# Counts of edges in fp16 with two loads on their way, and all products of codes on VectorE: a graph layer on one core of Trainium2

## What is computed

```python
xn = layernorm(x)
deg_inv = 1 / max(segment_sum(ones, dst), 1)
sage(h) = h @ W_self + (segment_sum(h[src], dst) * deg_inv) @ W_neigh + b
gnn = sage1(relu(sage0(xn)))
Q, K, V = elu(xn@Wq+bq)+1, elu(xn@Wk+bk)+1, xn@Wv+bv
mix = gelu((Q * sum(K*V) / (Q * sum(K) + 1e-6)) @ Wo + bo)
x1 = x + gnn + mix
h = act_qdq(layernorm(x1))             # act_qdq: rounding to 16-bit codes, one scale for the whole tensor
up, gate = act_qdq(h @ qdq(w_up).T), act_qdq(h @ qdq(w_gate).T)
gate = act_qdq(gate * round_u16(sigmoid(gate)))
out = x1 + act_qdq(gate * up) @ qdq(w_down).T
```

## Time and profile before

| | us |
|---|---|
| median of 3 runs | 1245.42 |
| lowest, highest | 1242.05, 1246.09 |
| the profiled execution | 1242.91 |
| its span, first to last instruction | 1241.1 |
| TensorE busy in it | 1161.6 |
| granted TensorE clock, mean | 0.972 |

### The profile page before, as it was taken

The page is one execution under the profiler, slowest core; times in us unless marked ns, Lnnn a source line. Parts: engine busy times, 40 slices in busy tenths (PEclk is TensorE's granted clock), DMA queues, the critical chain, the costliest instruction groups (busy, mean ns, idle before and its releaser), DMA issues.

```text
span 1241.1 us, 15392 instructions
## 1 busy us (share of the span) xinstructions
PE 1161.6 (94%) x6376; PEld 626.5 (50%) x6376; DVE 683.4 (55%) x1225; ACT 355.5 (29%) x442; POOL 385.5 (31%) x213
## 2 busy tenths in 40 slices
PE   3969999999999999999999999999999999979848
PEld 2535455555555554444444555444444445469724
DVE  6569578665373583227334344666655355662653
ACT  5443333323333323312421122312110022243430
POOL 2047576768777685786000000000000000000010
PEclk8879999999999999999999999999999999989969
DMA  9963554342433437526670135213130130000004
GB/s 283 393 212 53 156 112 122 63 107 20 90 53 56 107 70 249 147 44 216 237 259 3 59 113 178 85 35 136 69 102 17 46 142 1 1 1 2 1 31 135
DMA packets 140718, 130.33 MB, mean 105 GB/s; under 512 B 74892, under 2 KB 114060, under 8 KB 139624
## 3 DMA queue, kind: packets, MB, share of 16 engines
q1 hardware_dynamic: 72072, 116.24, 27.8%
q0 software_dynamic: 68288, 12.98, 8.0%
q10 hardware_dynamic: 288, 0.13, 0.0%
HBM read 101.25 MB, written 27.72 MB: 104 GB/s over the span
## 4 chain that ended last, share of the span: by engine, by line
PE 45%; DMA 23%; POOL 13%; issue 12%; DVE 3%; ACT 2%; SPq 1%; POOLq 0%; DVEq 0%; ACTq 0%
PE ps L1035 21%; DMA at_scratch<-copies,cell 16%; POOL at_scratch L597 12%; PE ps L1097 7%; PE ps L1069 7%; PE ps L1122 6%; PE ps L1142 3%; DMA at_scratch<-zeros 3%; DMA raw<-in_L_gnn_W_neigh_dram 2%; DMA raw<-in_L_gnn_W_self_dram 1%; DMA parts<-at_scratch 1%; DVE AT L1240 1%; PE ps L1014 1%; SPq L398 1%; PE ps L1085 1%
## 5 line engine op out<-in xcount | busy, mean ns | idle before, releaser
L952 PE MATMUL ps<-xnT,whl 128*128 128x512 f16 (+1 forms) x2160 | 386.4, 342 | 13.1 <-ACT Qs L762 10.6
L597 POOL DMA_INDIRECT at_scratch<-copies,cell x160 | 342.0, 2137 | 176.1 <-DMA at_scratch<-copies,cell 93.5
L952 PEld LDWEIGHTS ps<-xnT,whl 128*128 128x128 f16 x2160 | 211.7, 99 | 185.6 <-issue 15.8
L1035 PE MATMUL ps<-hb,hT 128*128 128x512 f16 x960 | 209.1, 379 | 1.4 <-DVE hT L1493 1.4
L1035 PEld LDWEIGHTS ps<-hb,hT 128*128 128x128 f16 x960 | 93.6, 98 | 112.3 <-DVE hT L1493 1.8
L579 POOL PARTITION_ALL_REDUCE ag_fw<-am_fw x9 | 3.2, 354 | 369.2 <-DVE am_fw L1360 369.2
L1035 PE MATMUL ps<-hb,xnT 128*128 128x512 f16 x480 | 105.9, 383 | 0.0
L1035 PE MATMUL ps<-hb,VT 128*128 128x512 f16 x480 | 103.9, 379 | 1.5 <-ACT S_b L721 1.5
L1097 PE MATMUL ps<-P,AT 125*128 125x512 f16 x400 | 87.8, 379 | 0.0
L1069 PE MATMUL ps<-AT,P 125*128 125x512 f16 (+1 forms) x480 | 84.7, 339 | 0.0
L1122 PE MATMUL ps<-codeT,w 128*128 128x250 f16 x600 | 67.5, 275 | 9.5 <-DVE codeT L1613 7.6
(11 more groups left out here) (224 smaller groups left out, 1181.1 us busy)
## 6 DMA issues: line engine op xcount, KB each, us to landing
raw<-in_L_gnn_W_neigh_dram SPq DMA_DIRECT2D x32, 512.0 KB, 5.9
parts<-at_scratch SPq DMA_DIRECT2D x20, 625.0 KB, 5.0
raw<-in_L_gnn_W_self_dram SPq DMA_DIRECT2D x24, 512.0 KB, 5.5
at_scratch<-zeros POOLq DMA_DIRECT2D x12, 1020.0 KB, 18.7
key_b<-key_scratch SPq DMA_DIRECT2D x8, 1250.0 KB, 11.2
raw<-in_L_mix_Wo_dram SPq DMA_DIRECT2D x16, 512.0 KB, 3.8
x_all<-in_x_dram SPq DMA_DIRECT2D x9, 512.0 KB
x_acc<-in_x_dram SPq DMA_DIRECT2D x9, 512.0 KB
```

The source lines that it names most:

```text
L597: pool.indirect_dma_start(out=at_scr[c % 2][:, :], out_offset=bass.IndirectOffsetOnAxis(ap=cell[:, c:c + 1], axis=0), in_=copies[:, c:c + ...
L952: mm = pe.matmul(acc_of(c)[:, a:b], whl[:, i, wp, k, :], xnT[:, k, ap, a:b], start=(k == 0 and wp == 0 and ap == 0), stop=(k == KC - 1 and ...
L1035: mm = pe.matmul(half_bank(i), stationary[:, k, ap, t * TP:t * TP + P], hb[:, n % 2, k, wp, :], start=(k == 0 and wp == 0 and ap == 0), st ...
```

## The change

- at_scr, zeros, parts and copies are fp16. The tile zeros keeps its bytes, so three DMAs clear an array, not six.
- cells(p) counts to a new fp32 tile, counted. One more VectorE instruction for each p writes copies: the number where it is under 255.5, otherwise 0, as 256 and more would not stay exact in fp16 sums.
- There are four part tiles. Parts 0 to 5 alternate between two tiles over AT's tiles 6 to 9; parts 6 to 9 alternate between two over b1_b and bo_b. Load 1 waits for nothing, loads 2 to 5, 8 and 9 for the add of the part two before, load 6 for b1_ok as before, load 7 for VectorE's last mix_in. counts(6) and counts(8) wait for the add before them, since they write over a part tile.
- POOL makes no product. ACT codes blocks 1 and 2 of U in one step each (round_code), and VectorE multiplies all three blocks.

```diff
--- before.py
+++ after.py
@@ -49,7 +49,7 @@
     NPC = 8
     CPP = ET // NPC
     CELLS = P * 12240
-    NZ = 6
+    NZ = 3
     IC = I // P
     BLK = 32
     NBLK = D // BLK
@@ -146,8 +146,9 @@
         w_last = sb("w_last", [P, 2, D], F16, RG)
 
 
-        zeros = sb("zeros", [P, CELLS // (NZ * P)], F32, RD)
-        parts = [sb("parts0", [P, 2, NP], F32, RG), sb("parts1", [P, 2, NP], F32, RD + 6 * NP * 2)]
+        zeros = sb("zeros", [P, CELLS // (NZ * P)], F16, RD)
+        parts = [sb(f"parts{q}", [P, 2, NP], F16, o) for q, o in enumerate(
+            (RD + 6 * NP * 2, RD + 8 * NP * 2, RG, RG + NP * 4))]
 
         edge = Area(RG, RG + 5024)
         e_int = edge("e_int", [EH, 4, EP], I32)
@@ -158,6 +159,7 @@
         once = kept("once", [EP, EP], F32)
         again = kept("again", [EP, CPP], F32)
         spare = kept("spare", [EP, CPP], F32)
+        counted = kept("counted", [EP, CPP], F32)
         squared = kept("squared", [P, D], F16)
 
         key_b = sb("key_b", [P, 2, CPP * EP], F32, RE + 8192)
@@ -203,7 +205,7 @@
         stats2 = const("stats2", [P, 2, 6], F32)
         amax2 = const("amax2", [P, 2, NT + 1], F32)
         spare_c = const("spare_c", [EP, 1], F32)
-        copies = const("copies", [EP, ET], F32)
+        copies = const("copies", [EP, ET], F16)
         cell = const("cell", [EP, ET], I32)
 
         ps = ctx.enter_context(nc.psum_tensor("ps", [P, 4096], F32))
@@ -218,7 +220,7 @@
         s_scr = nc.dram_tensor("s_scratch", (D, N), F32, kind="Internal").ap()
         diag_scr = nc.dram_tensor("diag_scratch", (P * (P + 1),), F32, kind="Internal").ap()
         key_scr = nc.dram_tensor("key_scratch", (E,), F32, kind="Internal").ap()
-        at_scr = [nc.dram_tensor(f"at_scratch{b}", (CELLS, 1), F32, kind="Internal").ap() for b in range(2)]
+        at_scr = [nc.dram_tensor(f"at_scratch{b}", (CELLS, 1), F16, kind="Internal").ap() for b in range(2)]
         w_scr = nc.dram_tensor("w_scratch", (NF, P, 2 * D), F16, kind="Internal").ap()
 
         def sem(name):
@@ -235,7 +237,7 @@
         zero_out, key_out = [sem("zero_out0"), sem("zero_out1")], sem("key_out")
         key_in = [sem("key_in0"), sem("key_in1")]
         scattered = [sem("scattered0"), sem("scattered1")]
-        parts_in = [sem("parts_in0"), sem("parts_in1")]
+        parts_in = [sem(f"parts_in{q}") for q in range(4)]
         out_done = sem("out_done")
 
         diag_set, diag_out, ident_in = sem("diag_set"), sem("diag_out"), sem("ident_in")
@@ -272,7 +274,6 @@
         ug_done, ug_free = sem("ug_done"), [sem("ug_free0"), sem("ug_free1")]
         g_step, g_round, gs_step, gs_round, u_step, u_round, o_step, o_round = (
             sem(n) for n in ("g_step", "g_round", "gs_step", "gs_round", "u_step", "u_round", "o_step", "o_round"))
-        u_last = sem("u_last")
         gate_ok, sig_ok, o_code, o_hi, o_lo = (sem(n) for n in ("gate_ok", "sig_ok", "o_code", "o_hi", "o_lo"))
         dn_done, dn_free = sem("dn_done"), sem("dn_free")
 
@@ -380,7 +381,7 @@
 
         def part_of(s):
 
-            return (1, s) if s < 6 else (0, s - 6)
+            return (s % 2, s // 2) if s < 6 else (2 + s % 2, (s - 6) // 2)
 
         def half_index(w, part):
             return HALVES.index((w, part))
@@ -511,8 +512,10 @@
                         sp.wait_ge(scattered[b], 16 * (ET // 2))
                 elif s == 6:
                     sp.wait_ge(b1_ok, NT)
-                else:
-                    sp.wait_ge(at_ok, s)
+                elif s == 7:
+                    sp.wait_ge(m1_ok, 2 * NT)
+                elif s != 1:
+                    sp.wait_ge(at_ok, s - 1)
                 for b in range(2):
                     sp.dma_start(parts[q][:, b, 0:N],
                                  at_scr[b][s * TP * N:(s * TP + P) * N, :].rearrange("(p n) o -> p (n o)", n=N)
@@ -605,13 +608,8 @@
                 pool.tensor_tensor(x_acc[:TP, t, :], x_acc[:TP, t, :], b1_b[:TP, :], ALU.add).then_inc(b1_ok, 1)
             for j in range(NF):
                 ffn_max(j)
-            for e in (X2, MG, MGS, MU):
+            for e in (X2, MG, MGS, MU, MO):
                 whole(e)
-
-            c = IC - 1
-            pool.wait_ge(u_round, 1)
-            pool.tensor_tensor(G[:, cols(c)], U[:, cols(c)], G[:, cols(c)], ALU.mult).then_inc(u_last, 1)
-            whole(MO)
 
         @block.scalar
         def _(act):
@@ -886,12 +884,7 @@
             ug_out(2 * NR_F - 2)
             ug_out(2 * NR_F - 1)
             act.wait_ge(u_step, 1)
-
-            c = IC - 1
-            steps(act.activation(U[:, cols(c)], U[:, cols(c)], ACT.Identity, bias=pos_magic[:, :],
-                                 scale=sv[:, Q_U + 1:Q_U + 2]))
-            act.activation(U[:, cols(c)], U[:, cols(c)], ACT.Identity, bias=neg_magic[:, :]).then_inc(u_round, 1)
-            for c in range(1, IC - 1):
+            for c in range(1, IC):
                 round_code(U[:, cols(c)], Q_U, u_round)
             act.wait_ge(o_step, 1)
             for r, (a, b) in enumerate(OCOLS):
@@ -1222,11 +1215,12 @@
                     c = p * CPP + q
                     keys = key_b[:EP, p % 2, q * EP:(q + 1) * EP]
                     last = dve.scalar_tensor_tensor(keys, keys, key_c[:, c:c + 1], once[:, :], ALU.is_equal,
-                                                    ALU.mult, accum_out=copies[:, c:c + 1])
+                                                    ALU.mult, accum_out=counted[:, q:q + 1])
                 last.then_inc(key_used, 1)
                 dve.wait_ge(key_used, p + 1)
                 of = slice(p * CPP, (p + 1) * CPP)
-                dve.tensor_scalar(again[:, :], copies[:, of], 255.5, None, ALU.is_ge)
+                dve.tensor_scalar(again[:, :], counted[:, :], 255.5, None, ALU.is_ge)
+                dve.scalar_tensor_tensor(copies[:, of], counted[:, :], 255.5, counted[:, :], ALU.is_lt, ALU.mult)
                 steps(dve.tensor_scalar(spare[:, :], key_c[:, of], -1.0, spare_c[:, 0:1], ALU.mult, ALU.add))
                 steps(dve.tensor_tensor(spare[:, :], spare[:, :], again[:, :], ALU.mult))
                 dve.tensor_tensor(cell[:, of], spare[:, :], key_c[:, of], ALU.add).then_inc(cell_ok, 1)
@@ -1234,8 +1228,8 @@
             def counts(s):
 
                 q, k = part_of(s)
-                if s == 6:
-                    dve.wait_ge(at_ok, 6)
+                if s in (6, 8):
+                    dve.wait_ge(at_ok, s - 1)
                 dve.wait_ge(parts_in[q], 32 * (k + 1))
                 dve.tensor_tensor(AT[:, s, 0:N], parts[q][:, 0, 0:N], parts[q][:, 1, 0:N], ALU.add).then_inc(at_ok, 1)
                 if s == NT - 1:
@@ -1664,14 +1658,11 @@
                                     ALU.mult, ALU.mult))
             steps(dve.tensor_scalar(sv[:, TMP2:TMP2 + 1], sv[:, TMP:TMP + 1], 1 / 32767.0, None, ALU.mult))
             for c in range(IC):
-                if c + 1 < IC:
-                    if c > 0:
-                        dve.wait_ge(u_round, c + 1)
-                    code(U[:, cols(c)], Q_U, rounded=c > 0)
-                    steps(dve.scalar_tensor_tensor(G[:, cols(c)], U[:, cols(c)], MAGIC, G[:, cols(c)], ALU.subtract,
-                                                   ALU.mult))
-                else:
-                    dve.wait_ge(u_last, 1)
+                if c > 0:
+                    dve.wait_ge(u_round, c)
+                code(U[:, cols(c)], Q_U, rounded=c > 0)
+                steps(dve.scalar_tensor_tensor(G[:, cols(c)], U[:, cols(c)], MAGIC, G[:, cols(c)], ALU.subtract,
+                                               ALU.mult))
                 last = max_of(G, c)
             steps(last)
             whole_max(MO, omax[:, 2, 0:IC])
```

## The result

| | before | changed |
|---|---|---|
| median, us | 1245.42 | 1231.20 |
| lowest, highest of 5 | 1240.55, 1250.19 | 1230.02, 1232.56 |
| span of the profiled execution, us | 1241.1 | 1229.1 |

The ratio is 0.9891, with a 95% interval of 0.9859 to 0.9923: 1.1% faster. The forecast was 1237, or 8.4 us less; 14.2 us went. The range, from 1231 to 1243, held it by 0.2 us. Two things stand out beside the size: the two profiled executions differ by 12.0 us, more than the sum of 8.3 made against them, and the changed kernel's five runs lie within 2.5 us where those of before spread over 9.6.

The account below looks back on a forecast made before the run. TensorE, busy 94% of the span, was taken as the bound, so only its stops and slow restarts pay. -5.0 - 3.5 + 0.2 = -8.3 us from 1242.91 gives 1234.6, plus 2.5 for the median: 1237; range 1231 to 1243.

Parts of the forecast that it names:

- The last product: Last layer, TensorE's stop of 21.6 us: all products on VectorE and no slow all-reduce on POOL save 5.0 us.
- rival 3: Last layer: POOL's all-reduce is slow without the product too; 4.23 us stay, 1241.2 us; chance 0.04.
- The loads: Loads of the counts: TensorE's 2.0 us stop at W_neigh1's column sum and the slow clock behind it go, 3.5 us.
- So the scatter's end has 7.0 us to spare: At tile 19, which needs a bank given back at 562.3 but begins near 569.3: the scatter could end 7.0 us later.
- a load that waits for the add two parts back: Part loads of the counts: no longer held by the add just before, so W_neigh1's rows come earlier; within the 3.5 us.
- hidden in both cases: VectorE's adds of count halves: 1.46 us is the upper end for fp16, and their time doesn't show.
- rival 4: First 80 us: the lighter DMA load helps there as well, by up to 4 us, 1233 us; chance 0.06.
- The start: Two added small VectorE instructions ahead of the weight scales and ACT's Qs: 0 to 0.5 us more, 0.2 taken.
- The scatter: Edges' scatter on POOL: keeps 160 instructions at 2.14 us mean; 2-byte accumulates land in 3.8 us as before, no change.
- rival 1: Scatter's pair rule at L596: 2-byte accumulates land later, the scatter ends later; 1260.5 us at 1.2 us later; chance 0.09.
- point of decision: Scatter's landing: decides from 0.9 us later on, as TensorE pays all beyond 7.0 + 1.5 = 8.5 us.
- Rival 2: Stop at L931 stays or turns into another; only the last product gains, 1240.6 us; chance 0.13, half a partial loss.

Follow-up runs that it names:

- e1: The kernel before with only the new last layer (VectorE makes all three products, POOL none): 1240.75 us, ratio 0.9954 to the kernel before.
- e2: The changed kernel with the old last layer (POOL makes block 2's product again): 1235.89 us, ratio 0.9917 to the kernel before.
- e8: The kernel before with six more memsets on POOL ahead of the last scatter, 10.8 us: 1258.0 us, ratio 1.0113 to the kernel before.
- e7: The changed kernel with three more memsets on POOL ahead of the last scatter, 10.5 us: 1238.51 us, ratio 0.9954 to the kernel before.
- e10: e7 with the old waits, each part loaded only when the part before it has been added: 1237.72 us, ratio 0.9940 to the kernel before.
- e11: The changed kernel with cells(0) and cells(1) behind the first weight scales and low halves of chunks 2 and 3: 1232.12 us, ratio 0.9889.
- e12: e10 with each add of two halves made by scalar_tensor_tensor, one element a cycle: 1247.64 us in a single run.
- e5: The changed kernel with the old waits, each part loaded only when the part before it has been added: 1232.23 us, ratio 0.9912.
- e9: The changed kernel with only cells(1) behind the first weight scales and low halves of chunks 2 and 3: 1225.36 us, ratio 0.9860.
- e6: The changed kernel clearing two more arrays, so as many bytes are zeroed as before; scatters wait for all: 1231.78 us in a single run.

## Why the prediction was right, and where it was not

**The last product: right.** The step gave 5.0 us; the traces show 16.6 us before the last product in all ten traces with the edit, and 21.1 to 21.8 in the four without it (21.6 in the first trace), so 4.5 to 5.2. e1 alone gave 5.7 us, with an interval that holds it. POOL's all-reduce starts at once when no product comes between: rival 3 falls.

**The loads: the term was mis-sized, and its reason was half wrong.** The step took 3.5 us from one trace: the stop of 1.95 us and the slow clock behind it. For that trace it was right, as e2's trace with the same W shows. But the metric is the median, and in it the term is 10.1 us by e2. Traced again, the old kernel has stops of 1.98 and 6.82 us, and e1 of 3.12, 2.51 and 4.92. What failed is the sentence "So the scatter's end has 7.0 us to spare". It was right of tile 19 in that trace, as no stop was there. But the time was already bound to the scatter through the ten loads, SP's queue and the rows of W_neigh1 behind them: S to degrees is 96.3 to 97.8 us in all four traces with the old loads, and in e8 a later scatter came through whole. TensorE's wait was small in the first trace since TensorE itself had come late, at 522.6. The view that said so was the chain of waits, which the prediction set aside. TensorE has 45 to 52% of it in the eight traces where S to degrees stands at 96 to 98, at 90.9 or at 86 us (the old loads, e7, e10, e11, e12), and 87 to 90% in the six where W to degrees is 119.4.
The prediction also laid part of the gain to a load that waits for the add two parts back. By e5 and e10 that is worth nothing once the parts are halved. The halved bytes do some 7 us and the faster adds, which the prediction called hidden in both cases, some 5, both read where the scatter's end sets the time. The adds were hidden from TensorE, but they lie in the chain that each next load waited for. The first pair's load shrank by 2.3 us (5.9 to 3.6), where the prediction took 1.5. Its estimate by the Trainium skill (DMA: Bandwidth & Descriptors, "Anatomy of one DMA"), 4.9 to 3.5 us, used a rule which that section gives for DMAs that GpSimd issues, while SP issues these; the median time to landing of one load was 5.0 us before and 3.3 in the changed kernel.

**The number.** The median fell inside the range by luck: the lower edge of 1231 was set for rival 4 with a low median, and rival 4 did not come true. Of the 12.0 us between the two first traces, 2.8 lie before W, 3.9 from W to the degrees and 5.0 before the last product. The 2.8 are chance too: W comes anywhere from 515.7 to 522.6 in the old kernel and e1, and from 517.6 to 522.7 in the changed kernel and e2. The old kernel ends by S and the changed one by W, so the changed one keeps an early TensorE. The spread of the runs fits: 2.5 to 5.7 us from lowest to highest in the changed kernel, e2, e5 and e9, and 8 to 17 in before, e1, e7, e10 and e11, all bound by the scatter. e8, bound by it too, is the exception, with 2.8 us in four runs.

**The start: +0.2 us taken, 0 to 0.5 as the range.** The wait for Qs is 10.1 to 10.8 us in four traces with the old cells, and 11.0 in seven with the new at their old place (10.7 in e6): some 0.5, the upper end.

**The scatter: right.** 2 bytes or 4, POOL's 2.13 us and its waits for landings are the same, and rival 1 falls. Its point of decision was not 8.5 us of room, though: e7 shows some 4 in the changed kernel. The Trainium skill (DMA: Bandwidth & Descriptors, "How a descriptor splits into AXI transactions") counts a transfer in beats of 32 B from a 256-byte boundary on, by which a cell of 2 and one of 4 bytes at the same place cost the same beats. The traces agree: 2130 and 2137 ns, and 96.0 and 93.5 us of waits for landings. Rival 2, a gain of the last layer only, falls too. Rival 4's time (1233) is nearer to the result than the forecast, but not for its reason (e6).

**What stays open.** Why the granted clock of the first 60 us differs between executions, and why the last scatter starts anywhere from 544.3 to 554.0 us in kernels that don't delay it, was not tried. The split of the loads' gain in bytes and adds rests on single traces. No run has two loads on their way with fp32 parts, so what they would have brought alone isn't shown.

## What to carry to other kernels

When an engine is busy for 94% and its waits are short, the end can still be set by something else: look whether the chain of waits runs elsewhere, and measure from its last event to the next mark in several traces, since a distance that stays while the busy engine comes early or late tells which sets the time. And an operation hidden behind another engine's work is not free where a DMA waits for it: the adds here took 0.65 us less each, and the end moved by some 5 us. A cost read from one trace holds for that execution; the median can gain three times as much.

## What the runs showed of the hardware that was not expected

- POOL started late whenever it changed between tensor_tensor and partition_all_reduce in the last layer, in both directions. From MODIFY_POOL_CONFIG to the start it was 6.9 and 5.7 us by the earlier trace rows (1177.2 to 1184.11, 1187.2 to 1192.89). By when the operands were ready, near 1180.4 and at 1188.6, it cost 3.7 and 4.3 us. With all-reduces alone it starts 0.25 us after VectorE's row begins.
- VectorE's adds of two halves ran longer beside POOL's additions of b1. The first fp16 add took 2.24 us in the changed kernel, and most later ones 0.80. In all 14 traces the adds that began while POOL was in the middle of its additions took longer, 1.6 to 2.8 us in fp16 and 2.4 to 2.7 in fp32 (2.57 at 582.26 in the first trace of before), and no other did (0.79 to 0.81; 1.44 to 1.46 in fp32 and in e12). No run moved POOL's additions, so this is read from when they ran and was not tried.
- POOL's memset of as many bytes took 1.80 us as 128 x 2040 fp32 and 3.50 as 128 x 4080 fp16, so its time went with the elements and not with the bytes.
- The same 12 matmuls behind the same idle time of 2.3 us took 4.45 and 2.76 us in two executions of one kernel, with a granted clock of 0.50 (50 to 52 us) and 1.00.
